# Batch 0's extra keys as 32-bit products, seven of its head norms on two other engines, and the first lookup chunk compared ahead of the scores

## What is computed

```python
x = x + _L0_xattn_ref(_layernorm(x, axis=-1), ctx_1024, ...)
x = x + _L0_ffn_ref(_layernorm(x, axis=-1), L0_ffn_lut, L0_ffn_gate_idx, L0_ffn_up_idx, L0_ffn_down_idx)
...
kv_dca = (y_dca @ Wkv_dca + bkv_dca).reshape(b, DCA, 2, H, HD)
k_dca = _ln(kv_dca[:, :, 0], kn_dca_w, kn_dca_b)
v_dca = kv_dca[:, :, 1]
q = _ln((x @ Wq + bq).reshape(b, s1, H, HD), qn_w, qn_b)
...
ctx = _attn(qT, k.transpose(0, 2, 1, 3), v.transpose(0, 2, 1, 3))
ctx_dca = _attn(qT, k_dca.transpose(0, 2, 1, 3), v_dca.transpose(0, 2, 1, 3))
```

## Time and profile before

| | us |
|---|---|
| median of 3 runs | 808.67 |
| the runs | 807.60 to 809.32 |
| the profiled execution's own time | 808.67 |
| its span | 806.4 |
| TensorE busy (matmuls) | 759.6 |
| VectorE busy | 509.5 |
| ScalarE busy | 492.5 |
| GpSimd busy | 254.5 |

### The profile page before, as it was taken

How to read it: one execution, slowest core, us unless ns; L and a number is a source line. 1 busy time by engine, 2 the same in 40 slices (tenths; PEclk the granted TensorE clock), 3 DMA queues, 4 the chain that set the end, 5 groups by cost and what they waited for, 6 DMA issues and landing times.

```text
span 806.4 us, 14838 instructions
## 1 busy us (share of the span) xinstructions
PE 759.6 (94%) x5842; PEld 311.6 (39%) x5842; DVE 509.5 (63%) x991; ACT 492.5 (61%) x1001; POOL 254.5 (32%) x267
## 2 busy tenths in 40 slices
PE   2888786999999999999999999999999999999998
PEld 1342232333443343234443343235433433365445
DVE  7979999898877994215769952238499800153211
ACT  3479889788646886663658866636488855511100
POOL 6883221000763321004843320036522200014320
PEclk9998999899999999999999999999999999999999
DMA  7749998586320001222400003222000000100001
GB/s 254 194 126 273 255 261 211 141 185 159 122 68 1 1 2 34 73 53 62 122 4 1 2 23 71 53 66 55 1 1 1 2 27 28 40 14 1 0 14 40
DMA packets 74244, 61.22 MB, mean 76 GB/s; under 512 B 33408, under 2 KB 60800, under 8 KB 73920
## 3 DMA queue, kind: packets, MB, share of 16 engines
q1 hardware_dynamic: 73840, 60.02, 28.0%
q10 hardware_dynamic: 208, 0.26, 0.1%
q0 software_dynamic: 128, 0.00, 0.0%
HBM read 43.29 MB, written 10.55 MB: 67 GB/s over the span
## 4 chain that ended last, share of the span: by engine, by line
PE 81%; DVE 12%; ACT 3%; issue 2%; POOL 1%; DVEq 0%; POOLq 0%; ACTq 0%
PE ps L1677 54%; PE ps L2028 8%; PE ps L2009 6%; PE ps L1980 5%; PE ps L1728 5%; DVE arena L1122 4%; DVE nmax L1472 3%; PE ps L1876 2%; ACT ps L1005 2%; PE ps L2015 2%; DVE nmax L1477 1%; DVE arena L1129 1%; POOL hrstd L684 0%; DVE stat L1159 0%; ACT arena L808 0%
## 5 line engine op out<-in xcount | busy, mean ns | idle before, releaser
L1677 PE MATMUL ps<-arena,wf_hi 128*128 128x512 f16 (+2 forms) x736 | 211.0, 371 | 0.7 <-issue 0.7
L1005 ACT ACTIVATE ps<-ps,nmax 128x496 f32<-128x496 f32 x256 | 166.2, 652 | 23.1 <-DVE nmax L1477 23.1
L1037 ACT ACTIVATE arena<-ps 128x1024 f32<-128x1024 f32 x128 | 124.3, 1026 | 72.1 <-PE ps L2015 72.1
L1677 PE MATMUL ps<-arena,wf_lo 128*128 128x512 f16 (+2 forms) x368 | 136.1, 370 | 0.0
L1677 PE MATMUL ps<-wf_hi,arena 128*128 128x512 f16 (+3 forms) x374 | 114.8, 368 | 0.4
L684 POOL TENSOR_TENSOR hrstd<-hvar,mhalf 128x16 f32<-128x16 f32 (+1 forms) x33 | 101.3, 3086 | 40.5 <-DVE hvar L1226 40.3
L1677 PEld LDWEIGHTS ps<-arena,wf_hi 128*128 128x128 f16 (+1 forms) x736 | 69.6, 100 | 85.6 <-issue 21.6
L1122 DVE TENSOR_SCALAR arena<-arena,wf_lo 128x2048 f16<-128x2048 f16 (+1 forms) x132 | 89.5, 739 | 5.6 <-PE ps L1728 5.4
L633 POOL TENSOR_TENSOR xrstd<-xvar,mhalf 128x1 f32<-128x1 f32 x32 | 23.9, 746 | 206.9 <-DVE xvar L1164 206.9
L1728 PE MATMUL ps<-arena,wf_lo 128*32 128x512 f16 (+1 forms) x1056 | 66.4, 396 | 13.5 <-ACT arena L832 9.5
L1677 PE MATMUL ps<-wf_lo,arena 128*128 128x512 f16 (+3 forms) x187 | 68.5, 366 | 0.0
(11 more groups left out here) (153 smaller groups left out, 1039.9 us busy)
## 6 DMA issues: line engine op xcount, KB each, us to landing
arena<-idx SPq DMA_DIRECT2D x124, 128.0 KB, 3.6
arena<-in_x SPq DMA_DIRECT2D x32, 256.0 KB, 2.9
wf_lo<-in_idx SPq DMA_DIRECT2D x10, 512.0 KB, 5.1
idx<-wf_hi SPq DMA_DIRECT2D x10, 384.0 KB, 4.3
out<-arena SPq DMA_DIRECT2D x15, 256.0 KB, 2.0
wf_lo<-in_idx SPq DMA_DIRECT2D x11, 256.0 KB, 6.3
arena<-in_ctxT SPq DMA_DIRECT2D x5, 512.0 KB, 3.7
v_next<-arena SPq DMA_DIRECT2D x8, 256.0 KB, 4.4
```

The source lines that it names most:

```text
L1005: last = act.activation(sc, sc, ACT.Exp, bias=nmax[:, 0, t, h:h + 1], accum_out=den[:, 0, t, h:h + 1])
L1037: act.activation(probs[n_ % 2][:, 2 * p:2 * p + 2, :], ps[:, bank:bank + 2, :], ACT.Exp).then_inc(s["probs_set"], 1)
L1677: last = pe.matmul(dst, l, r, start=(first and i == 0), stop=(stop and i == len(todo) - 1))
```

## The change

- The extra rows' keys and values are multiplied in 32 bits: `product` gets plain operands (`ctx_dca`, scaled by 256 in place by ACT, and `st_d` as loaded). The centring moves behind the product: `extra_centre` works on the 64 x 512 result in PSUM. Gone are ACT's split of Wkv_dca (L972) and of the 16 extra rows (L961), and DVE's four helpers for them.
- In batch 0 units 0 to 6 get one over the square root from DVE's `reciprocal` (`inverse`) and ACT's `Sqrt` (`root`). Units 7 and 8 keep `rstd` on POOL. POOL converts the first two index blocks earlier.
- Chunk 0 is compared before the scores (four `one_hot` calls between the last units). Its `look_up` also waits until all nine units are rescaled, since unit 8 is turned in bank 7, which `look_up` uses (`turn_bank`).
- Unit 8 is normalised after the maximum of step 1 (was 0), turned after `scores(2)` (was `scores(0)`), rescaled after step 1's exponentials; `scores(2)` waits for eight units, not nine.
- The lists before the scores are reordered on PE, ACT and DVE, and the load of Wo waits for the last extra product instead of `wd_lo`, since it lands in the same place.

The core of the diff (context lines left out):

```diff
@@ -434,8 +435,6 @@
...
-            sp.wait_ge(s["wd_lo"], 1)
-            sp.dma_start(st_o.rearrange("p (k n) -> p k n", k=G), by_chunk("Wo")).then_inc(s["wo_in"], 16)
@@ -460,6 +459,8 @@
...
+            sp.wait_ge(s["v_done"], nth_value((0, 0), len(values_of((0, 0)))))
+            sp.dma_start(st_o.rearrange("p (k n) -> p k n", k=G), by_chunk("Wo")).then_inc(s["wo_in"], 16)
@@ -680,15 +681,23 @@
...
+                    if prev is None:
+                        pool.wait_ge(s["hrstd_set"], u)
...
-                    rstd(0)
+                    norm(1, 0, (0, 0))
+                    selectors()
+                    norm(1, 1, (0, 0))
+                    norm(1, 2, (0, 0))
...
-                    for u in range(1, len(units)):
-                        rstd(u)
+                    norm(1, 3, (0, 0))
...
+                    lookup_constants()
+                    shift_patterns()
+                    rstd(7)
+                    rstd(8)
@@ -837,6 +838,8 @@
...
+                elif units_of(a)[u][0] == "d":
+                    act.wait_ge(s["kd_cent"], 1)
@@ -846,6 +849,13 @@
...
+            def root(u):
+                n_ = MD if UNITS_0[u][0] == "d" else P
+                act.wait_ge(s["inv_set"], u + 1)
+                if u >= 2:
+                    act.wait_ge(s["qn_set"], u - 1)
+                act.activation(hrstd[0:n_, u % 2, :], hinv[0:n_, u % 2, :], ACT.Sqrt).then_inc(s["hrstd_set"], 1)
+
@@ -949,42 +959,47 @@
...
+                    act.wait_ge(s["wv_in"], 16)
+                    act.activation(fl(wv[0]), st_kv[1], ACT.Copy, scale=WS).then_inc(s["wv_hi"], 1)
+                    query_hi(2)
...
-                    query_hi(2)
...
-                    act.wait_ge(s["wv_in"], 16)
-                    act.activation(fl(wv[0]), st_kv[1], ACT.Copy, scale=WS).then_inc(s["wv_hi"], 1)
+                    context_hi(a, ctx_first, cT)
...
-                    act.activation(cd[0].rearrange("p k n -> p (k n)"), ctx_dca, ACT.Copy).then_inc(s["cd_hi"], 1)
-                    context_hi(a, ctx_first, cT)
+                    act.activation(ctx_dca, ctx_dca, ACT.Copy, scale=WS).then_inc(s["cd_hi"], 1)
+                    act.wait_ge(s["wk_cent"], 1)
+                    act.activation(fl(wk[0]), st_kv[0], ACT.Copy, scale=WS).then_inc(s["wk_hi"], 1)
...
-                    act.wait_ge(s["wk_cent"], 1)
-                    act.activation(fl(wk[0]), st_kv[0], ACT.Copy, scale=WS).then_inc(s["wk_hi"], 1)
+                    root(0)
...
+                    root(1)
+                    values(0)
...
-                    values(0)
-                    act.wait_ge(s["wd_cent"], 1)
-                    act.activation(wd[0][:, :, :], st_d, ACT.Copy, scale=WS).then_inc(s["wd_hi"], 1)
-                    values(1)
-                    turn(1, 2, LB0[2])
+                    root(2)
...
+                    turn(1, 2, LB0[2])
+                    root(3)
+                    root(4)
+                    values(1)
...
+                    rescale(2)
...
-                    rescale(2)
-                    values(2)
+                    square(a, 6, True)
...
-                    square(a, 6, True)
+                    root(5)
...
+                    root(6)
...
+                    values(2)
@@ -1004,7 +1019,7 @@
...
-                    if prev is None and m == 0:
+                    if prev is None and m == 1:
@@ -1224,6 +1239,13 @@
...
+
+            def inverse(u):
+                n_ = MD if UNITS_0[u][0] == "d" else P
+                dve.wait_ge(s["hsum_set"], u + 1)
+                if u >= 2:
+                    dve.wait_ge(s["hrstd_set"], u - 1)
+                dve.reciprocal(hinv[0:n_, u % 2, :], hvar[0:n_, u % 2, :]).then_inc(s["inv_set"], 1)
@@ -1398,70 +1420,78 @@
...
+                    inverse(6)
+                    one_hot(0, (0,))
+                    one_hot(0, (1,))
+                    low_half(5)
-                    low_half(5)
-                    variance(a, 8)
+                    one_hot(0, (2,))
+                    variance(a, 8)
+                    value_bias()
+                    one_hot(0, (3,))
@@ -1587,27 +1617,14 @@
...
-            dk = st_d.rearrange("p k (n h d) -> p k n h d", n=2, d=HD)[:, :, 0]
-
-            def extra_sums():
-                dve.wait_ge(s["wd_in"], 16)
-                dve.tensor_reduce(sum_d, dk, AX_X, ALU.add).then_inc(s["wd_sum"], 1)
-
-            def extra_centre():
-                dve.wait_ge(s["wd_sum"], 1)
-                for k in range(KC):
-                    last = dve.scalar_tensor_tensor(out=dk[:, k], in0=spread(sum_d[:, k, :]), scalar=-1.0 / HD, in1=dk[:, k],
-                                                    op0=ALU.mult, op1=ALU.add)
-                last.then_inc(s["wd_cent"], 1)
-
-            def extra_low():
-                dve.wait_ge(s["wd_hi"], 1)
-                low(wd[1][:, :, :], st_d, wd[0][:, :, :]).then_inc(s["wd_lo"], 1)
-
-            def extra_context_low():
-                dve.wait_ge(s["cd_hi"], 1)
-                dve.tensor_tensor(cd[1].rearrange("p k n -> p (k n)"), ctx_dca, cd[0].rearrange("p k n -> p (k n)"),
-                                  ALU.subtract).then_inc(s["cd_lo"], 1)
+            def extra_centre(a):
+                u = units_of(a).index(("d", 0))
+                kd_ps = heads(ps[0:MD, proj_bank(a, u), :])
+                dve.wait_ge(s["proj_done"], nth_unit(a, u + 1))
+                dve.tensor_reduce(sum_d, kd_ps, AX_X, ALU.add).then_inc(s["kd_sum"], 1)
+                dve.wait_ge(s["kd_sum"], 1)
+                dve.scalar_tensor_tensor(out=kd_ps, in0=spread(sum_d), scalar=-1.0 / HD, in1=kd_ps, op0=ALU.mult, op1=ALU.add)\
+                    .then_inc(s["kd_cent"], 1)
@@ -1632,7 +1649,7 @@
...
-                    if c < NCH - 1:
+                    if 0 < c < NCH - 1:
@@ -1721,6 +1738,8 @@
...
+                if not c:
+                    pe.wait_ge(s["tr_hi"], len(UNITS_0))
@@ -1834,10 +1853,10 @@
...
-                        pe.wait_ge(s["cd_lo"], 1)
-                        pe.wait_ge(s["wd_lo"], 1)
+                        pe.wait_ge(s["cd_hi"], 1)
+                        pe.wait_ge(s["wd_in"], 16)
...
-                        keys = [(both(lambda a_: cd[a_][:, i, :]), both(lambda a_: wd[a_][:, i, 0:D])) for i in range(KC)]
+                        keys = [(ctx_dca[:, i * MD:(i + 1) * MD], st_d[:, i, 0:D]) for i in range(KC)]
@@ -1873,7 +1892,7 @@
...
-                        last = pe.transpose(ps[:, TB + u % 2, g * P:g * P + n_], qn[u % 2][0:n_, g * P:(g + 1) * P], ident[0:n_, 0:n_])
+                        last = pe.transpose(ps[:, turn_bank(u), g * P:g * P + n_], qn[u % 2][0:n_, g * P:(g + 1) * P], ident[0:n_, 0:n_])
@@ -1901,26 +1920,30 @@
...
-                else:
+                elif prev is not None:
...
+                    turn(1, 0, a, LB0[0], x_first[0])
+                    turn(1, 1, a, LB0[1], x_first[1])
+                    project(0)
+                    project(1)
+                    project_values(0)
...
+                    project_values(1)
...
-                    project_values(0)
...
-                    project_values(1)
...
-                    project_values(2)
...
+                    project_values(2)
+                    project(6)
+                    turn_heads(3)
...
-                    turn_heads(3)
-                    project(6)
@@ -1970,7 +1993,7 @@
...
-                        pe.wait_ge(s["tr_hi"], nth_unit(a, len(units)))
+                        pe.wait_ge(s["tr_hi"], nth_unit(a, len(units) - (prev is None)))
@@ -1986,7 +2009,7 @@
...
-                    if prev is None and m == 0:
+                    if prev is None and m == 2:
```

90 lines of the change are left out of this document (42 added, 48 removed).

## The result

The changed kernel takes 810.65 us (median of 11 runs, 809.96 to 814.24), the kernel before 808.22 (11 runs, 807.40 to 810.07) on the same chip: a ratio of 1.0036, 95% interval 1.0026 to 1.0047. It is slower, by 2.4 us in the medians. The forecast of 808.2 and its range up to 810.3 were wrong. The profiled execution has a span of 808.7 us against 806.4, +2.3.

What follows compares the result with a forecast made beforehand. It took GpSimd's norms and TensorE's work, nearly equal, to bound the stretch before the scores, VectorE the score loop, TensorE the rest. Terms -1.3 + 0.7 + 0.1 = -0.5 us from 808.67 gave 808.2 us, range 805.6 to 810.3.

Steps and rivals of the forecast that it cites:

- Term B: Start of scores (S) to chunk 1's comparisons (the mark): 9.9 us at half clock, 9.19 before, so +0.7 us.
- Term C: Chunk 1's comparisons follow look_up(0) quarter by quarter at half clock: +0.1 us taken, up to 0.4.
- What bounds the kernel: Before the scores, GpSimd's norms and TensorE's work, nearly equal; in the score loop VectorE; after 141 us TensorE.
- Term A: Before the score loop: moving seven of nine powers off GpSimd starts the scores at 53.5, 1.3 us earlier.
- I find most of them closed: Before the scores: most of TensorE's holes, 0.90 + 0.51 + 0.88 + 0.46 = 2.75 us, would close.
- The conversions beside VectorE: Before the scores: two index conversions, 1.46 us each, slow neighbouring VectorE work; at most 1.5 us in the bounds.
- after that a pair of steps costs VectorE what it cost before: In the score loop after chunk 1's comparisons: VectorE's cost per pair of steps stays unchanged.
- Transfers, "covered": At the loop's entrance: Wo's and the next context's loads land by S+8.3, thinly covered; late, under 1 us.
- The slower one: Entrance becomes the bound, scores start at 55.3 or later, mark at 65.6: +1.6 us, 810.3; chance 0.15.
- The faster one: All holes before the scores close and TensorE keeps its clock at the entrance: -2.5 us, 806.2; chance 0.28.

Runs made afterwards that it cites:

- experiment 6: The changed kernel with eighteen unread products on TensorE between scores(0) and scores(2), in the hole at the loop's entrance: 808.87 us, ratio 1.0007 to the kernel before.
- experiment 7: The changed kernel with unit 8 turned between scores(0) and scores(2), not behind scores(2): 811.00 us, ratio 1.0037 to the kernel before.
- 4: The changed kernel with the exponentials' table loaded early, by a one-column exponential on ScalarE before square 8: 811.13 us, ratio 1.0032 to the kernel before.
- experiment 5: The changed kernel with twelve unread products on TensorE before the first value product, in the hole of 3.33 us: 809.93 us, ratio 1.0021 to the kernel before.
- Experiments 1: The changed kernel with unit 8's low half on GpSimd moved right behind the third index conversion: 809.42 us, ratio 1.0012 to the kernel before.
- 14: The changed kernel with late x loads, unit 8's low half early and unit 8 turned before scores(2), without filling products: 807.69 us, ratio 0.9986 to the kernel before.
- experiment 3: The kernel before with only Wo's load issued late, beside the next context's: 808.21 us, ratio 0.9997 to the kernel before.
- experiment 2: The changed kernel with two loads of the next batch's x issued at chunk 16 instead of chunk 4: 811.15 us, ratio 1.0032 to the kernel before.
- 13: The changed kernel with late x loads, unit 8's low half early, unit 8 turned before scores(2), and 25 unread filling products: 805.28 us, ratio 0.9968 to the kernel before.
- experiment 15: The changed kernel with late x loads, low half early, unit 8 turned before scores(2), 25 filling products and ten more: 805.53 us, ratio 0.9963 to the kernel before.

## Why the prediction was wrong

**The sum.** Forecast: -1.3 + 0.7 + 0.1 = -0.5. The profiled execution: -1.36 up to the scores, +1.31 to the mark, +0.53 in the quarters, +2.44 in the rest of the loop, -0.65 after it, +2.3 in all. The term that was missing is the 2.44; terms B and C were too small by 0.6 and 0.4.

**What bounds the kernel**: right. What follows the loop did not change beyond its scatter.

**Term A** (scores at 53.5): right at 53.45, in executions without the clock spell, but not by the way that I gave. Between the query products and the scores TensorE's holes are 3.33 + 0.61 us, more than the 2.75 before. The number came out since the reordered query products end at 23.68 us and not at 27.23; that balance is luck. The 32-bit products cost 0.89 us more than the 16-bit ones (0.84 said). Reciprocal and root are 0.24 and 0.22 us (0.2 assumed):

```profile
26.77 0.24 DVE L1248 RECIPROCAL hinv<-hvar 128x16 f32<-128x16 f32 x1
...
29.26 1.04 DVE L1184 TENSOR_SCALAR arena<-arena,mv,xrstd 128x512 f32<-128x512 f32 x1
...
36.73 1.61 DVE L1270 TENSOR_TENSOR arena<-arena 128x512 f16<-128x512 f32 x1
```

So the step "I find most of them closed", said of TensorE's holes, **failed**. Of the small ones one of 0.61 us is left, and one of 3.33 us opened before the first value product, because VectorE now subtracts for Wv and Wk back to back (1.22 and 1.23 us, and the context's 1.21 behind them) before TensorE may start. My forecast names no such hole, and did not ask what one does to the clock. In the median of the change it costs little, as its profile shows; it makes the upper four of eleven times. The price stands in the profiles of the experiments: the scores start at 54.80 where the clock was half until about 30 us (6), at 56.04 and 56.77 where it was until 32 and 33 (7, 4), and at 53.30 where it held (5). The conversions beside VectorE cost what I had bounded: 0.50 us on the `standardise` at 29.26 (1.04 where its like took 0.54) and 0.93 on the low half at 36.73 (1.61 for 0.68). The exclusive lock of the Trainium skill, "SBUF — State Buffer", in its part on the port pair, agrees with the low half (two inputs in SBUF). The `standardise` and the comparisons in the loop have one input and were held up as well; the same part of the Trainium skill names a second case, VectorE's two-port performance modes, which no row here can confirm.

**Term B** (S to mark 9.9 us): 10.50, in the right order and with the half clock as taken. Its own terms add up to 9.78 (5.0 + 1.4 + 1.11 + 1.45 + 0.82), and to 8.42 at full clock, not to 9.9 and 8.6. The table load took 1.28 us, and the exponential started right behind it, at 57.12; `scores(2)` began 0.24 us later behind the exponentials than I gave it, and the first comparison 0.34 us later behind the first quarter. With the clock held it is 8.97 (experiment 6).

**Term C** (+0.1, at most 0.4): 0.5 at 69 us. Its last sentence, "after that a pair of steps costs VectorE what it cost before", is the step that **failed** most clearly, and the one that made the forecast wrong: 2.4 us of the profiled execution arise at 84 to 98 us, 1.07 in comparisons beside a conversion and 1.37 in `look_up(5)` at half clock. I had read no row of that stretch, so I missed that ScalarE's early value already waited 1.21 us there for GpSimd, at the end of a chain that starts with a transfer of indices. Experiments 1 and 14 show it from the other side: with the low half early the loop from the mark to its end takes 77.03 and 76.81 us, before 77.06, in the change 80.00.

**Transfers, "covered"**: right for Wo and the context, which nobody waited for (experiment 3), wrong for the indices in the same queue. The sixth conversion's took 9.0 us to landing in place of 6.3, so they landed at about 83.9 us and not at 80.7, and the conversion started 2.3 us later. Why is open: Wo's move alone gave 7.2 us (experiment 3), the late loads of x brought them to 7.4 (experiment 2).

**Rivals.** The slower one had the right sign and nearly the right time (810.3) by the wrong way: the scores did not start late, and the entrance only took back what they had gained (mark at 63.95 for 64.00). The faster one's condition, a clock held at the entrance, is what experiments 6 and 13 made by hand. The chance of 0.15 for slower was too small because both failed steps could only cost, and neither had a share.

## What to carry to other kernels

A new order is to be read for the holes that it makes on TensorE, not for their sum alone: a hole of 3 us can put half clock on what follows, in some executions only, and then the times fall into groups while the profile shows one of them. A few products that nobody reads held the clock through such a hole in every profile, and cost nothing that could be seen; the next unfilled hole can still take it (13). When work on an engine off the path moves, follow its queue to the end of the stage, with every wait in it of over a microsecond that others stand behind, even where the change touches nothing.

## What the runs showed of the hardware

The price of half clock at 27 us is what the slowed products lose, carried on undiminished for 20 us. Against experiment 5, TensorE's first transposes behind the projections start 1.51 us later in experiment 6 (33.96 for 32.45), the scores 1.50. In experiment 7 it is 2.75 and 2.74. The half clock lasted until about 30 us in the first and until about 32 in the second. With the holes filled (experiment 15) TensorE's clock never fell in the score loop, where it had been 0.92 in the change:

```profile
53.28:139.50 86.22, 65.19 (x776) 24.19 (x775) 82.86 (x108) 79.16 (x221) 23.84 (x19) 1.00 0.99 258
```

VectorE's comparisons take longer with an index conversion of GpSimd beside them (3.79 for 2.72 us in the change, 3.94 in experiment 6). In experiment 7 it was the other way: the conversion started in the last comparison and took 2.32 us, the comparisons 2.73. VectorE's maxima, read from PSUM, do not take longer: 2.27 to 2.29 us with a conversion beside them, in every trace.
